# A DLRM tower on one core: five features per row give six pair products and a square, and the gathers are paced by layer-1 steps

## The reference

```python
e = stack([tbl_f[ids[:, f]] for f in range(39)], axis=1)    # 512 x 39 x 16
for W in (W0, W1):                                          # (39*39, 128), (39*128, 128)
    z = einsum('bmd,bnd->bdmn', X0, Xi)                     # X0 = e; Xi = e, then the layer before
    Xi = einsum('bdp,po->bod', z.reshape(b, d, -1), W)
z = concat(both Xi, axis=1).sum(-1)                         # 512 x 256
h = relu(concat([z, dense]) @ W_top1 + b_top1)              # 272 -> 512
h = relu(h @ W_top2 + b_top2)                               # -> 256
y = h @ W_top3                                              # -> 1
```

## Time and profile before

| | us |
|---|---|
| median of 3 runs | 264.42 (264.13 to 265.26) |
| the profiled execution, its own time | 262.94 |
| its span, first to last instruction | 260.9 |

### The profile page before, as it was taken

How to read it: one execution, slowest core, us unless ns; L and a number is a source line. 1 busy time by engine, 2 the same in 40 slices (tenths; PEclk the granted TensorE clock), 3 DMA queues, 4 the chain that set the end, 5 groups by cost and what they waited for, 6 DMA issues and landing times.

```text
span 260.9 us, 5243 instructions
## 1 busy us (share of the span) xinstructions
PE 235.9 (90%) x1848; PEld 182.4 (70%) x1848; DVE 196.1 (75%) x341; ACT 168.6 (65%) x324; POOL 128.8 (49%) x180
## 2 busy tenths in 40 slices
PE   4998856989799978939999999999999999999996
PEld 4997733555466754737777777777787888898795
DVE  1799969998879999556889999879989877624001
ACT  4997555675787886547759878686757655466203
POOL 4788888888888888878888882000000000000000
PEclk9999755899999999988999999999999999999999
DMA  5920001545026540200221111010110101010000
GB/s 160 233 45 10 9 5 13 112 83 129 8 27 147 122 96 7 28 8 9 45 33 20 24 11 28 5 25 7 21 16 12 25 1 25 4 25 0 3 0 0
DMA packets 30883, 10.30 MB, mean 39 GB/s; under 512 B 21018, under 2 KB 30138, under 8 KB 30858
## 3 DMA queue, kind: packets, MB, share of 16 engines
q1 hardware_dynamic: 27722, 9.17, 16.3%
q0 software_dynamic: 3136, 0.81, 3.5%
HBM read 7.34 MB, written 0.00 MB: 28 GB/s over the span
## 4 chain that ended last, share of the span: by engine, by line
PE 48%; POOL 26%; DVE 12%; issue 9%; ACT 3%; DMA 2%; DVEq 0%; ACTq 0%
POOL feat L355 21%; PE s_bank L964 11%; POOL pad L353 5%; PE b_bank L904 4%; PE l_bank L925 4%; PE l_bank L927 4%; PE l_bank L926 4%; DVE z L716 3%; DVE w_sb L660 3%; DVE z_lo L730 3%; PE g_bank L949 2%; PE g_bank L950 2%; PE g_bank L951 2%; PE xi_bank L934 1%; ACT g L448 1%
## 5 line engine op out<-in xcount | busy, mean ns | idle before, releaser
L355 POOL DMA_INDIRECT feat<-tbl,ids_sb x98 | 107.3, 1095 | 29.4 <-POOL pad L353 21.1
L716 DVE TENSOR_TENSOR z<-xa,b_bank 128x512 f32<-128x512 f32 (+1 forms) x112 | 76.1, 684 | 17.3 <-PE b_bank L904 13.8
L529 ACT ACTIVATE z_hi<-z 128x512 fp32r<-128x512 f32 (+1 forms) x104 | 65.6, 630 | 18.9 <-DVE z L716 17.5
L730 DVE TENSOR_TENSOR z_lo<-z,z_hi 128x512 fp32r<-128x512 f32 x88 | 60.3, 686 | 0.0
L904 PE MATMUL b_bank<-xs,sel 117*128 117x512 bf16 (+1 forms) x112 | 45.2, 406 | 8.7 <-DVE z L716 8.6
L964 PE MATMUL s_bank<-g,w_sb 128*128 128x128 f32 x312 | 46.3, 278 | 0.0
L964 PEld LDWEIGHTS s_bank<-g,w_sb 128*128 128x128 f32 x312 | 42.2, 192 | 1.3 <-issue 0.7
L925 PE MATMUL l_bank<-z_hi,w_hi 128*128 128x512 f32 x88 | 41.8, 474 | 0.0
L904 PEld LDWEIGHTS b_bank<-xs,sel 117*128 117x128 bf16 (+1 forms) x112 | 11.5, 103 | 38.3 <-DVE z L716 20.7
L537 ACT ACTIVATE g<-g_bank 128x320 f32<-128x320 f32 x64 | 27.7, 432 | 16.3 <-PE g_bank L951 16.0
L927 PE MATMUL l_bank<-z_hi,w_lo 128*128 128x512 f32 x88 | 35.1, 399 | 0.0
(11 more groups left out here) (190 smaller groups left out, 368.2 us busy)
## 6 DMA issues: line engine op xcount, KB each, us to landing
diag<-xt SPq DMA_DIRECT2D x128, 20.0 KB
w_sb<-w SPq DMA_DIRECT2D x3, 832.0 KB
feat<-tbl,ids_sb POOLq DMA_INDIRECT x98, 2.4
wt_sb<-wt SPq DMA_DIRECT2D x2, 512.0 KB, 4.7
g<-small SPq DMA_DIRECT2D x1, 770.0 KB
g<-small SPq DMA_DIRECT2D x1, 448.0 KB
w0p<-w_pair SPq DMA_DIRECT2D x1, 448.0 KB
w0m<-w_mirror SPq DMA_DIRECT2D x1, 448.0 KB
```

The source lines that it names most:

```text
L355: nc.gpsimd.indirect_dma_start(feat[:, bt % 2, n * D:(n + 1) * D], None, tables[order[n]], bass.IndirectOffsetOnAxis(ids_sb[:, bt, order[n ...
L529: nc.scalar.activation(z_hi[0:rows, s % RING, :], z[0:rows, at, :], ACT.Copy).then_inc(rounded, 1)
L716: nc.vector.tensor_tensor(target, xa[0:rows, bt % 2, c * CB:(c + 1) * CB, :].rearrange("p b d -> p (b d)"), b_bank[s % B_RING][0:rows, :], ...
L730: nc.vector.tensor_sub(low[first:rows, s % RING, :], z[first:rows, SPLITS[s] % Z_RING, :], z_hi[first:rows, s % RING, :].bitcast(f32)).the ...
```

## The change

**Factors.** Each of the 128 rows now holds five features instead of a fixed first and seven second ones: two stand in `factors` (a and b, SBUF), three are selected into `b_bank`. Steps 0 to 5 of a chunk multiply the a and b factor with each of the three selected banks, two products to a bank (2 x 3 = 6); step 6, `REST_T`, multiplies a with itself, which gives the 39 squares. The table of features (`BASES`, `CHAIN`) covers the 741 pairs of unlike features with these. So a chunk has three selects where it had seven, and two fills (`fill_a`, `fill_b`) where it had one; step 6 uses all 128 rows and no selected bank. Its weights have the high or the low part by row (two DVE operations in place of three copies).

**Order.** `LEAD` is 2: PE issues a select at every second step, up to two steps ahead. `fill_b` of the next chunk comes at step 3 of a chunk in `xi_bank`, `fill_a` stays at step 4 in `turn_bank`; ACT makes both copies (`take_factor`), but for the first b, which DVE copies. The b-factor of a tile's first chunk comes at `B_AT`. `Z_RING` is 6, `factors` a ring of 3 chunks. `SPLIT_AT`, `X_AT` and `A_AT` of tile 2 and `SPLIT_AT[3][2]`, `A_AT[3]` are moved. `split_w0` goes ahead of DVE's first `take_x`.

**Gathers.** The fills of `pad` are gone. From the 31st gather on, each waits for one more layer-1 step: gather number n (from 0) waits until `l1_used` is n - 29.

```diff
-PT = -(-PAIRS // P)
-REST = PAIRS - (PT - 1) * P
-REST_AT = (0, F, 2 * F)
-REST_LO = 64
-REST_ROWS = 96
-ROWS = [P] * (PT - 1) + [REST_ROWS]
-assert REST <= F and REST_AT[1] >= 32 and REST_AT[1] + REST <= REST_LO <= REST_AT[2] and REST_AT[2] + REST <= REST_ROWS
+PT = 7
+REST_T = PT - 1
+REST_LO = slice(64, 64 + F)
+SELECTS = 3
+BASES = ((0, 5, 10, 13, 20), (0, 14, 3, 16, 21), (0, 8, 12, 14, 17))
+CHAIN = (1, 3, 0, 2, 4)
+LEAD = 2
...
-Z_RING = Z_LAG + 2
-LEAD = 1
+Z_RING = 6
+F_RING = 3
 RING = LAG + 2
+assert RING == PT
...
-REST_COLS = 192
 FREE_FIRST = 8
+PACED_FROM = 30
...
+FILL_B = 3
...
-SPLIT_AT = [[], [8, 14, 19], [8, 14, 19], [9, 16, 21]]
-X_AT = [[], [21, 22], [21, 22], [23, 24]]
-A_AT = [0, 24, 24, 26]
+SPLIT_AT = [[], [8, 14, 19], [9, 16, 22], [9, 16, 22]]
+X_AT = [[], [21, 22], [23, 24], [23, 24]]
+A_AT = [0, 24, 25, 25]
+B_AT = [0, 25, 26, 26]
...
-        xa = sb("xa", [P, 2, P, D])
-        sel = sb("sel", [R, PT + 1, P], bf16)
+        factors = sb("factors", [P, F_RING, 2, CH])
+        sel = sb("sel", [R, SELECTS + 2, P], bf16)
...
-        turn_banks = [turn_bank, xi_bank, l1_bank[1]]
+        turn_banks = [turn_bank, xi_bank, l1_bank[1], b_bank[1]]
...
-        fills = [[("x", 0, 0)], [("x", 0, 1)], [("a", 0, 0)]]
+        fills = [[("x", 0, 0)], [("x", 0, 1)], [("a", 0, 0)], [("b", 0, 0)]]
...
+            if (i := chunk_at(s, FILL_B)) is not None and (i + 1) % CPT:
+                fills[1].append(("b", i + 1, 0))
...
+            if bt + 1 < TILES and v == B_AT[bt + 1]:
+                fills[1].append(("b", CPT * (bt + 1), 0))
...
-                        if bt:
-                            fills_done += 1
-                            nc.gpsimd.memset(pad[:], 0.0).then_inc(rested, 1)
-                            pool.wait_ge(rested, fills_done)
+                        if bt and sent >= PACED_FROM:
+                            pool.wait_ge(l1_used, sent - PACED_FROM + 1)
...
-            def take_a(i):
-                bt, c = divmod(i, CPT)
-                act.wait_ge(*after(turn_filled, "a", i, 0))
-                k = fill["a", i, 0][0]
-                nc.scalar.activation(xa[:, bt % 2, c * CB:(c + 1) * CB, :],
-                                     turn_banks[k][:].rearrange("p (b d) -> p b d", d=D),
+            def take_factor(name, i):
+
+                act.wait_ge(*after(turn_filled, name, i, 0))
+                if i >= F_RING:
+                    act.wait_ge(product, PT * (i - F_RING + 1))
+                k = fill[name, i, 0][0]
+                nc.scalar.activation(factors[:, i % F_RING, "ab".index(name), :], turn_banks[k][:],
                                      ACT.Copy).then_inc(turn_taken[k], 1)
...
                 nc.vector.tensor_sub(w0_lo[:], w0p[:], w0_hi[:].bitcast(f32)).then_inc(w0_summed, 1)
+                high, low = (numbers[:, k:k + 1] for k in (sum(class_blocks), sum(class_blocks) + 1))
+                nc.vector.tensor_scalar(w0_rest[:], w0_hi[:, REST_T, :].bitcast(f32), high, None,
+                                        ALU.mult).then_inc(w0_split, 1)
                 dve.wait_ge(w0_summed, 2)
-                for lo in range(0, REST_ROWS, 32):
-                    w = w0_lo if lo == 32 else w0_hi
-                    nc.vector.tensor_copy(w0_rest[lo:lo + 32, :], w[lo:lo + 32, PT - 1, :]).then_inc(w0_split, 1)
+                dve.wait_ge(w0_split, 1)
+                nc.vector.scalar_tensor_tensor(w0_rest[:], w0_lo[:, REST_T, :].bitcast(f32), low, w0_rest[:].bitcast(f32),
+                                               ALU.mult, ALU.add).then_inc(w0_split, 1)
...
+            split_w0()
             take_x(0, CB, chunk0_taken)
-            split_w0()
+            dve.wait_ge(*after(turn_filled, "b", 0, 0))
+            nc.vector.tensor_copy(factors[:, 0, 1, :], b_bank[1][:]).then_inc(turn_taken[3], 1)
...
             def multiply(s):
-                i, t = divmod(s, PT)
-                bt, c = divmod(i, CPT)
-                rows = ROWS[t]
+                i, u = divmod(s, PT)
                 if direct(s):
                     number = s - SPLITS[s]
                     if number == 0:
                         dve.wait_ge(zeroed, 4)
                     if number >= WHOLE:
                         dve.wait_ge(l1_used, DIRECT_STEPS[number - WHOLE] + 1)
-                    target = whole[number % WHOLE][0:rows, :]
+                    target = whole[number % WHOLE][:]
                 else:
                     if SPLITS[s] >= Z_RING:
                         dve.wait_ge(remainder, SPLITS[s] - Z_RING + 1)
                         dve.wait_ge(rounded, SPLITS[s] - Z_RING + 1)
-                    target = z[0:rows, SPLITS[s] % Z_RING, :]
-                if t == 0:
-                    dve.wait_ge(*after(turn_taken, "a", i, 0))
-                dve.wait_ge(selected, s + 1)
-                nc.vector.tensor_tensor(target,
-                                        xa[0:rows, bt % 2, c * CB:(c + 1) * CB, :].rearrange("p b d -> p (b d)"),
-                                        b_bank[s % B_RING][0:rows, :], ALU.mult).then_inc(product, 1)
+                    target = z[:, SPLITS[s] % Z_RING, :]
+                k, j = u % 2, u // 2
+                if u < 2:
+                    dve.wait_ge(*after(turn_taken, "ab"[u], i, 0))
+                one = factors[:, i % F_RING, k, :]
+                if u == REST_T:
+                    other = one
+                else:
+                    dve.wait_ge(selected, SELECTS * i + j + 1)
+                    other = b_bank[(SELECTS * i + j) % B_RING][:]
+                nc.vector.tensor_tensor(target, one, other, ALU.mult).then_inc(product, 1)
...
+                low, rows = (z_lo, slice(0, P)) if s % PT != REST_T else (z_hi, REST_LO)
+                nc.vector.tensor_sub(low[rows, s % RING, :], z[rows, SPLITS[s] % Z_RING, :],
+                                     z_hi[rows, s % RING, :].bitcast(f32)).then_inc(remainder, 1)
...
-            def fill_a(i):
-
-                turn_free("a", i, 0)
+            def fill_factor(name, i):
+
+                turn_free(name, i, 0)
                 features_there(i)
-                k = fill["a", i, 0][0]
-                nc.tensor.matmul(turn_banks[k][:], sel[:, PT, :], columns(i // CPT, i % CPT),
+                k = fill[name, i, 0][0]
+                nc.tensor.matmul(turn_banks[k][:], sel[:, SELECTS + "ab".index(name), :], columns(i // CPT, i % CPT),
                                  start=True, stop=True).then_inc(turn_filled[k], 1)
...
-            def select(s):
-
-                i, t = divmod(s, PT)
-                bt, c = divmod(i, CPT)
-                if s >= B_RING:
-                    pe.wait_ge(product, s - B_RING + 1)
-                if t == 0:
+            def select(i, j):
+
+                q = SELECTS * i + j
+                if j == 0:
                     features_there(i)
-                nc.tensor.matmul(b_bank[s % B_RING][0:ROWS[t], :], sel[:, t, 0:ROWS[t]], columns(bt, c),
+                if q >= B_RING:
+                    before, number = divmod(q - B_RING, SELECTS)
+                    pe.wait_ge(product, PT * before + 2 * number + 2)
+                elif q == 1:
+                    pe.wait_ge(*after(turn_taken, "b", 0, 0))
+                nc.tensor.matmul(b_bank[q % B_RING][:], sel[:, j, :], columns(*divmod(i, CPT)),
                                  start=True, stop=True).then_inc(selected, 1)
...
-            fill_a(0)
-            for s in range(LEAD):
-                select(s)
+            fill_factor("a", 0)
+            fill_factor("b", 0)
+            select(0, 0)
             for s in range(LAST):
                 bt, v = divmod(s, SPT)
-                if s + LEAD < STEPS:
-                    select(s + LEAD)
+                i, u = divmod(s + LEAD, PT)
+                if i < CHUNKS and u in (0, 2, 4):
+                    select(i, u // 2)
```

## The result

The changed kernel takes 251.41 us, the median of 6 runs (250.67 to 255.21), beside 264.35 us (6 runs) of the kernel before on the same chips. The ratio is 0.9515, 95% interval 0.9479 to 0.9552: 4.9% faster, 12.8 us. The profiled execution took 252.58 us with a span of 250.7, so in the two profiles the gap is 10.2 us of span.

The account below looks back on a forecast made before the run. DVE was taken to bound early chunks, a late gather to stall chunk 6, PE to bound most later chunks. Span 260.9 - 7.5 - 6.2 + 2.6 = 249.8; from the median, 264.4 - 11.1 = 253.3 us, range 250 to 257.

Parts of the forecast that it names:

- gathers: Tiles 1 and 2: pacing removes the late-gather stalls, 6.1 us in chunk 6 and 1.4 at tile 1; -7.5 us.
- selects: Chunks 2 to 15: three fewer matmuls each at 0.24 us, capped at half of DVE's idle time; -6.2 us.
- edges of tiles 2 and 3: Starts of tiles 2 and 3: PE waits 1.0 us for b fill and copy, plus 0.3 for features, twice; +2.6 us.
- start, chunks 0 and 1: Start: split_w0 fits DVE's wait for transposes, b copy replaces three small copies; 0, bounds -1 and +1 us; selects there: nothing.
- The square: Step 6 of each chunk: 128 rows from SBUF instead of 96 from PSUM take DVE equally long; 0 us.
- The second factor: 15 more ACT copies, 0.6 us a chunk: hidden within a tile, but not at starts of tiles 2 and 3; +2.6 us.
- The signs: Profile after: first, no late gathers, chunk 6 near 12 us; second, shorter chunks 11 to 14; third, PE idle at tiles 2, 3.
- PE bounds everywhere: Rival, chance 0.18: chunks 2 to 14 all gain 0.72 us and tile edges lose nothing; 247.5 us.
- DVE taking over: Rival, chance 0.18: saved PE time becomes waits for DVE, only the gathers count, edges are paid; 259.5 us.
- Two products to a bank: Rival, chance 0.05: each chunk's third select makes PE wait 1.37 us for a multiply and subtraction; 275.2 us.
- The gathers are not late: Denies the rival, chance 0.04, that gathers stay late: stall returns at tile 2, appears at tile 3; 263.8 us.
- The clock: Rival, chance 0.05: PE stays at 1.2 GHz through chunks 1 to 3, costing about 3 us each; 262 us.

Follow-up runs that it names:

- e1: The kernel before with only the gathers changed: no fills, from the 31st each waits for one more layer-1 step; 256.09 us, ratio 0.9702.
- e3: The changed kernel with each of the 48 selects issued twice into the same bank; 255.41 us, ratio 0.967.
- e4: The changed kernel with the b-factor fill for the first chunk of tiles 2 and 3 one step earlier (25, not 26); 249.91 us, ratio 0.945.
- e10: The same edit to the changed kernel as e4, run in more rounds; 250.36 us, ratio 0.9458.
- e11: The changed kernel with LEAD 1 instead of 2 and four buffers of z instead of six; 251.72 us, ratio 0.9523.
- e8: The changed kernel with a further ACT copy of 384 columns ahead of each of the 15 b-factor copies; 253.8 us, ratio 0.9597.
- e2: The changed kernel with the fills of pad back ahead of the gathers of tiles 1 to 3 and no waits for layer-1 steps; 261.16 us, ratio 0.9813.
- e7: The changed kernel with DVE's subtraction for xit_lo one step later (REST_XI = TURN_XI + 2); 251.72 us, ratio 0.9523.
- e12: The changed kernel with tile 2's splits, transposes and first fills at the earlier kernel's steps, b factor early at tiles 2 and 3; 249.25 us, ratio 0.9424.
- e9: A variant whose profile is cited; the text given states neither its change nor its measured time.

## Why the prediction was right, point by point

The forecast was 253.3 us, the measured time 251.4, inside its own range of 250 to 257. The mechanism holds for the gathers, for the edges and for the price of one select. That the sum came so near is partly luck: the selects were put 2.8 us too high and about 1 us for ACT's copy was missing, and gains that no term foresaw made up for both. The terms:

| term | predicted | measured | from |
|---|---|---|---|
| gathers | -7.5 | -7.4 in the chunks, -7.9 in the median | e1 |
| selects | -6.2 | -3.4 in the chunks, -3.5 to -4.1 in the median | e3 |
| edges of tiles 2 and 3 | +2.6 | +1.9 in the chunks, +2.1 in the median | e4, e10 |
| rings | 0 | 0 | e11 |
| ACT's b copy elsewhere | 0 | about +1 | e8 |
| start, chunks 0 and 1 | 0 | -0.8 in the profiles, not settled | table |

**Gathers.** Right, with the mechanism. What I missed is that a gather wait costs more than its length: with the clock's fall 2 to 3 us of wait cost 5 (e2). The comparison with chunk 10 had that in it without my naming it.

**Selects.** The price of 0.24 us each is confirmed. The step that failed is the share in which it counts: half of DVE's idle time in the window of the kernel before was the wrong rule. It gave 0.7 to each of chunks 2, 6 and 10 and some tenths to 3 to 5 and 8, 2.9 us in all, and e3 shows nothing there. In chunks 6 and 10 DVE had no idle time left to give: in the changed kernel it is busy 11.87 of 12.1 us in each, with 23 operations in the window where there were 19. In chunk 2 neither engine is full (PE 10.03, DVE 10.20 of 11.9). In chunks 12, 13 and 14, where PE was busy throughout and DVE for 91%, 91% and 70%, the saving came in full (0.7, 0.6, 0.9 for 0.5, 0.5, 0.7). A full PE alone did not decide it: chunks 3 and 9 were full before too, with DVE at 96% and 99%, and the added matmuls cost 0 and 0.3 us there; chunk 10 was full but for 0.1 us, with DVE at 83%.

**Edges.** The wait was foreseen at its place, and it is 0.8 us idle (1.0 predicted) in the chunks that hold steps 55 and 83. At tile 1, with a step between, PE does not wait for this copy. Moving the fill gives back 1.9 us for two edges, so the 0.3 for the features' copy is not needed.

**The square.** Its duration from two SBUF inputs is 682 ns, with one PSUM input it is 679. By form, and the groups of the page that answer to the earlier trace rows:

```profile
L732 DVE TENSOR_TENSOR z<-factors 128x512 f32<-128x512 f32 x16 | 10.9, 682 | 0.0
```

```profile
L732 DVE TENSOR_TENSOR z<-factors,b_bank 128x512 f32<-128x512 f32 x96 | 64.8, 679 | 5.0 <-ACT factors L428 2.5
L742 DVE TENSOR_TENSOR z_lo<-z,z_hi 128x512 fp32r<-128x512 f32 x88 | 60.2, 684 | 3.4 <-ACT z_hi L532 3.4
...
L917 PE MATMUL b_bank<-xs,sel 117*128 117x512 bf16 x48 | 19.8, 413 | 3.0 <-DVE z L732 2.5
```

So the rule of the Trainium skill (VectorE: DVE Perf Modes, section on the TRN2 errata), by which the SBUF source would be 65 ns shorter, does not hold for `tensor_tensor` here, and the 0 stands.

**The second factor.** It was called hidden within a tile. e8 shows that it is in chunks 5, 6, 8 to 10 and 12 to 15, and not in 2 to 4: 1.1 us for an added copy of about 0.48 us. For the real one I estimate from this 1 us or a little more. In the table chunks 2 and 3 of the changed kernel are indeed 0.7 and 0.4 longer than those of e1; that these are the copy's is an inference from e8, not shown by a run without it. e7 fits it: in chunk 3 DVE waits 0.5 us for an ACT rounding, and without that wait the chunk is 9.1. Chunk 4 is 1.1 shorter than in e1; 0.4 of it is the moved split (10.0 in e12), the rest is not explained.

**The signs.** The signs of the first and the third term came as predicted. Of the second, chunks 12 to 14 came at 10.5, 10.9 and 13.1 us; chunk 11 came at 12.1 and not at 11.0, a figure from which the prediction had left out its own loss at the edge. One sign of being wrong did appear: DVE was to be over 90% busy in chunks 10 to 13, and it is at 98%, 78%, 88% and 96%. In chunk 12 that fits the whole 0.7 counting where 0.5 was allowed; in chunk 13, at 96%, it counted in full all the same, so the sign was no good measure. A small misreading beside it: DVE was busy 97% in chunk 8 of the kernel before, not 98%.

**What is open.** In the profiles the terms add up to -7.4 - 3.4 + 1.9 + 1.1 - 0.8 = -8.6 us (gathers, selects, edges, copy, start), and the gap is -10.2. The missing 1.6 us lie mainly in chunk 4 (1.1 shorter than in e1) and in chunks 8 to 10 (0.7 together). No run shows their cause; the new layout of the products and the moved order are untested there. The medians lie 12.8 us apart (ratio), with an interval of 1 us to either side, since the profiled execution of the kernel before was 1.5 below its median and that of the changed kernel (252.58) 1.2 above its own. The start (51 to 54 us, also for kernels that are the same there) and the clock in chunk 5 make single executions differ by more than that.

**The rivals.** That PE bounds everywhere is refuted by e3 (+3 to +4 us, not +11.5). DVE taking over is half true: it did where I allotted tenths, and in chunks 6 and 10, where I had put 0.7. Two products to a bank show no cost: at its selects' weight loads PE waits 7.1 us in all for products, against 20.7 before and 15.1 in e1, where no gather is late (the waits of the whole span). The gathers are not late. The clock was 0.63 in chunk 0, against 0.72 before, but it did not stay low in chunks 1 to 3 (1.00 in each).

## What to carry to other kernels

Price a removed matmul by the pitch of its neighbours, not by its duration. Where it counts is harder to see: a window in which the engine is busy throughout is not enough, if the next engine is at 96% there or has work that moves in. The cheap test is to put as many matmuls back and compare window by window. Tie a prefetch to the progress of its consumer rather than to time: the pace by fills became a stall in new places as soon as the rest got faster. And look at what stands first in the next step before placing a transfer of a shared bank last in a step; here one line was worth 2 us.

## What the runs showed of the hardware

The granted clock of PE made short stalls dearer. After windows in which PE was busy 0.86 and 0.10 of 2 us each, it was at 1.2 GHz for some 7 us, in which PE was busy nearly all the time, and a wait of DVE for a gather of 2.1 to 2.7 us went with a chunk 5.0 us longer (e2, twice in one execution, with the same size). The Trainium skill (TensorE: Matmul & The Clock Gate, part 1) calls the throttled state the default, which activity releases; the trace agrees in so far as the clock fell after PE had done little and came back after it had been busy. In chunk 5 the clock fell in the profiles of e4, e7 and e10 and not in those of the changed kernel and of e9, with nearly the same work: whether it falls differs between executions there, and it is worth 1.0 to 1.8 us.
